# One fp32 product with 136 columns turns a merged block and gives its router logits, and two pieces of TensorE's order move

## The reference

```python
# attention half, x is (8, 1024, 256)
g1 = sigmoid(out_swa @ lin1.T)
g2 = sigmoid(out_mem @ lin2.T)
x = x + (g1 * out_swa + g2 * out_mem)
# expert half
h = layernorm(x)
logits = h @ gate_w.T + gate_b            # 8 experts
topk_prob, topk_idx = top_k(softmax(logits), 2)
pos = cumsum(one_hot(topk_idx)) - 1       # place in the expert's buffer, 1280 places
# gather into the buffers, relu MLP of each expert, weighed sum back onto x
```

## Time and profile before

| | |
|---|---|
| median of 3 runs | 2372.16 us (2371.49 to 2372.21) |
| profiled execution | 2377.75 us, its span 2375.9 us |
| PE busy | 2334.7 us, 98% of the span |
| PE weight loads | 2081.5 us, 88%, beside the products |
| DVE busy | 1689.6 us, 71% |
| ACT busy | 1608.0 us, 68% |
| POOL busy | 1390.1 us, 59% |
| merge phase | about 1392 to 1912 us from the start of the span |

### The profile page before, as it was taken

The page is one execution under the profiler, slowest core; times in us unless marked ns, Lnnn a source line. Parts: engine busy times, 40 slices in busy tenths (PEclk is TensorE's granted clock), DMA queues, the critical chain, the costliest instruction groups (busy, mean ns, idle before and its releaser), DMA issues. The chain is left out here.

```text
span 2375.9 us, 40039 instructions
## 1 busy us (share of the span) xinstructions
PE 2334.7 (98%) x14847; PEld 2081.5 (88%) x14847; DVE 1689.6 (71%) x3668; ACT 1608.0 (68%) x2459; POOL 1390.1 (59%) x1000
## 2 busy tenths in 40 slices
PE   7999999999999999999999999999999899999999
PEld 6888888788888888888888978888888789999999
DVE  7777786666666666666666677777777757777776
ACT  4787888757777777777777657777777545555443
POOL 3565566566776666666667734666666553333433
PEclk9999999999999999999999999999999999999999
DMA  4222221543332223222233322333322055555651
GB/s 130 86 86 72 90 81 54 202 134 69 69 74 63 63 63 67 63 62 63 66 69 66 88 92 87 106 103 101 97 90 75 14 152 153 139 140 150 149 143 60
DMA packets 295394, 221.74 MB, mean 93 GB/s; under 512 B 189282, under 2 KB 262023, under 8 KB 295072
## 3 DMA queue, kind: packets, MB, share of 16 engines
q1 hardware_dynamic: 281376, 188.74, 29.3%
q0 software_dynamic: 13824, 30.44, 4.3%
HBM read 113.30 MB, written 72.12 MB: 78 GB/s over the span
## 5 line engine op out<-in xcount | busy, mean ns | idle before, releaser
L2780 ACT ACTIVATE e_hf<-e_ps_z,e_b 128x640 f32<-128x640 f32 x128 | 101.8, 795 | 211.9 <-PE e_ps_z L105 180.6
L2504 POOL TENSOR_TENSOR m_hl<-m_hf,m_hh 128x512 fp32r<-128x512 f32 x112 | 159.2, 1444 | 103.8 <-ACT m_hh L2103 102.4
L2908 POOL DMA_INDIRECT out<-e_ys,slot_token x80 | 83.2, 1040 | 218.8 <-DVE e_ys L2859 213.2
L105 PE MATMUL e_ps_y<-r_w_h,e_hl 128*128 128x256 f32 x640 | 180.6, 282 | 0.0
L105 PE MATMUL e_ps_y<-r_w_l,e_hh 128*128 128x256 f32 x640 | 179.2, 280 | 0.0
L105 PE MATMUL e_ps_y<-r_w_h,e_hh 128*128 128x256 f32 x640 | 178.9, 280 | 0.0
L1686 POOL TENSOR_TENSOR halves_l<-hT_full,halves_h 128x512 fp32r<-128x512 f32 x120 | 153.4, 1301 | 38.7 <-ACT halves_h L1337 38.7
L932 POOL DMA_INDIRECT xbuf_d<-xn,scatter_rows x128 | 135.8, 1061 | 57.7 <-issue 36.2
L789 POOL TENSOR_TENSOR prob<-prob,softmax_small 128x1024 f32<-128x1024 f32 x65 | 123.2, 1895 | 71.1 <-DVE softmax_small L705 71.1
L105 PE MATMUL e_ps_z<-slotsT_h,w_l 128*128 128x320 f32 x512 | 159.2, 311 | 2.1 <-DVE slotsT_l L2837 2.1
L105 PE MATMUL e_ps_z<-slotsT_l,w_h 128*128 128x320 f32 x512 | 159.1, 311 | 0.0
(11 more groups left out here) (371 smaller groups left out, 8969.5 us busy)
## 6 DMA issues: line engine op xcount, KB each, us to landing
shared_xT<-xT_d SPq DMA_DIRECT2D x64, 256.0 KB, 3.6
new_w1T<-in_W SPq DMA_DIRECT2D x16, 1024.0 KB
new_w2T<-in_W SPq DMA_DIRECT2D x16, 1024.0 KB
xbuf_d<-new_w1T SPq DMA_DIRECT2D x16, 650.0 KB, 8.4
shared_x<-in_x SPq DMA_DIRECT2D x16, 512.0 KB, 4.3
xn_d<-xn SPq DMA_DIRECT2D x32, 256.0 KB, 2.4
xT_d<-shared_xT SPq DMA_DIRECT2D x32, 256.0 KB, 2.6
oT_d<-shared_oT SPq DMA_DIRECT2D x32, 256.0 KB, 2.6
```

The costliest lines, as they stand in the source:

```text
L105: i = e.matmul(out, a, b, start=first and not onto and n == 0, stop=last and n == len(terms) - 1, skip_group_check=onto)
L2504: e.tensor_tensor(hl[:, t, 0:N], hf[(HC * C + t) % NZ][:, 0:N], hh[:, t, 0:N], ALU.subtract).then_inc(*h_low(C, t))
L2780: e.activation(hf[(HC * i + t) % NHF][:].rearrange("p (s n) -> p s n", s=2), ps_z[t % 2][:, :, 0:HALF], ACTF.Relu, bias=b1[:, i % E, t:t + ...
L2908: e.indirect_dma_start(io["out"], bass.IndirectOffsetOnAxis(ap=token[i % 2][:, b:b + 1], axis=0), ys[:, b], None, bounds_check=NT - 1, oob ...
```

## The change

The transposes and the small router products become one plain fp32 product for each of the 8 pairs of block and half. Its moving operand is a new tile `turned` (printed `ident_and_gate`): 128 columns of the identity and the 8 columns of the centred gate, for each half k. It writes 136 columns into a unit of 171 columns of a three-bank PSUM tile `m_ps_t`. The identity columns of a unit are the turned block; the 8 gate columns of the two halves have to be added, which DVE does with a new `sum_logits`. This holds for chunks 0 to 14. Chunk 15 keeps the old way.

Moved are: `residual_router(C-1)` stands behind `gate1(C)`, where `residual` and `router` stood ahead of it; `dispatch(C-2)` stands behind `memory_out(C, 0, 0)`, where it stood ahead of it; ACT's `copy_x1(C-1)` stands behind both `gate1` sigmoids. `dispatch(C)` on TensorE waits in addition for `x1_made` and `lg_summed` of the chunk behind. SP issues two more DMAs of the identity, behind the gate weights and ahead of the other constants.

```diff
         x2 = sb("xn2_full", [P, GRP, D])
-        gate_c, ones_f = sb("gate_centred", [P, KC, E]), sb("m_ones_f", [P, P])
+        turned = sb("ident_and_gate", [P, KC, P + E])
+        gate_c, ones_f = turned[:, :, P:], sb("m_ones_f", [P, P])
...
-        ps_r = ps("m_ps_r", [P, GRP, D])
-        ps_s = ps("m_ps_s", [P, 512])
-        ps_l, ps_c = ps_s[:, 0:GRP * E], ps_s[:, GRP * E:]
+        ps_t = ps("m_ps_t", [P, 3 * 512])
+        units = ps_t[:, 0:GRP * KC * UNIT].rearrange("p (j k x) -> p j k x", k=KC, x=UNIT)
+        ps_r = ps_t[:, 0:GRP * D].rearrange("p (j d) -> p j d", j=GRP)
+        ps_l, ps_c = ps_t[:, GRP * KC * UNIT:GRP * KC * UNIT + GRP * E], ps_t[:, GRP * KC * UNIT + GRP * E:]
...
-        merged_T, logits_done = (signal(n, tails) for n in ("merged_T", "logits_done"))
+        merged_T = signal("merged_T", tails)
+        logits_done = signal("logits_done", [u for u in tails if u[0] == NCH - 1])
+        turned_in = signal("m_turned_in", range(KC), 16)
+        lg_summed = signal("m_lg_summed", chunks[:-1])
...
+            def residual_router(C):
+                pe.wait_ge(*merged.at(C, 0))
+                for k in range(KC):
+                    pe.wait_ge(*turned_in.at(k))
+                pe.wait_ge(*gate_centred.at(0))
+                pe.wait_ge(*x1_made.at(*final_part(C - 1)))
+                if C:
+                    pe.wait_ge(*lg_summed.at(C - 1))
+                if C >= 2:
+                    pe.wait_ge(*placed.at(C - 2, 1))
+                for j in range(SIZES[C]):
+                    for k in range(KC):
+                        i = e.matmul(units[:, j, k, 0:P + E], ga[:, k, j * P:(j + 1) * P], turned[:, k], start=True, stop=True)
+                i.then_inc(*merged_T(C, 0))
...
-                pe.wait_ge(*lg_scaled.at(C))
+                if C < NCH - 1:
+                    read = min(C + 1, NCH - 2)
+                    pe.wait_ge(*x1_made.at(read, 0))
+                    pe.wait_ge(*lg_summed.at(read))
+                else:
+                    pe.wait_ge(*lg_scaled.at(C))
...
@@ -2059,15 +2087,14 @@
                     gate2(C - 1)
                 for t in range(2, HC):
                     hidden(C, t)
+                gate1(C)
                 if tail:
-                    residual(C - 1, 0)
-                    router(C - 1, 0)
-                gate1(C)
+                    residual_router(C - 1)
                 if C == 0:
                     sum_gate()
+                memory_out(C, 0, 0)
                 if sent:
                     dispatch(C - 2)
-                memory_out(C, 0, 0)
                 memory_out(C, 0, 1)
                 memory_out(C, 1, 0)
                 if C == NCH - 1:
...
-                e.activation(x1[s][:, blocks], ps_r[:, blocks], ACTF.Copy).then_inc(*x1_made(C, n))
+                if C < NCH - 1:
+                    e.activation(x1[s][:].rearrange("p j (k d) -> p (j k) d", k=KC),
+                                 units[:, :, :, 0:P].rearrange("p j k d -> p (j k) d"), ACTF.Copy).then_inc(*x1_made(C, n))
+                else:
+                    e.activation(x1[s][:, blocks], ps_r[:, blocks], ACTF.Copy).then_inc(*x1_made(C, n))
...
                 round_hidden(C, 6)
                 round_hidden(C, 7)
                 if tail:
-                    copy_x1(C - 1, 0)
                     gate1(C, 0)
                 gate1(C, 1)
+                if tail:
+                    copy_x1(C - 1, 0)
...
+            def sum_logits(C):
+                dve.wait_ge(*merged_T.at(C, 0))
+                dve.wait_ge(*x1_made.at(C, 0))
+                dve.wait_ge(*chosen.at(C - 1, 0))
+                dve.wait_ge(*shifted.at(C - 1, 0))
+                e.tensor_reduce(lg[:], units[:, :, :, P:P + E].rearrange("p j k x -> p j x k"), AX.X, ALU.add).then_inc(*lg_summed(C))
+
             def router(C):
                 n, wide = SIZES[C], [P, SIZES[C], E]
                 src = ps_l.rearrange("p (j x) -> p j x", x=E)
-                dve.wait_ge(*logits_done.at(*final_part(C)))
                 dve.wait_ge(*gate_b_in.at(0))
-                dve.wait_ge(*chosen.at(C - 1, 0))
-                dve.wait_ge(*shifted.at(C - 1, 0))
+                if C < NCH - 1:
+                    src = lg[:]
+                    dve.wait_ge(*lg_summed.at(C))
+                else:
+                    dve.wait_ge(*logits_done.at(*final_part(C)))
+                    dve.wait_ge(*chosen.at(C - 1, 0))
+                    dve.wait_ge(*shifted.at(C - 1, 0))
...
                 if tail:
+                    sum_logits(C - 1)
                     norm_stats(C - 1, 0)
                 if sent:
                     dispatch(C - 2)
...
             load_oT(0)
             load_x(0)
             e.dma_start(gate[:], io["gateT"].rearrange("(c p) n -> p c n", p=P)).then_inc(*gate_in(0))
+            for k in range(KC):
+                e.dma_start(turned[:, k, 0:P], io["ident"]).then_inc(*turned_in(k))
             e.dma_start(gate_b[:], io["gate_b"]).then_inc(*gate_b_in(0))
             e.dma_start(ident[:], io["ident"]).then_inc(*ident_in(0))
```

More of the change, by code:

```diff
@@ L1812, in gradient_phase @@
         sems.give_back(made)
+UNIT = 171
 def merge_banks():
```

## The result

| | before | after |
|---|---|---|
| median | 2371.35 us (10 runs, 2369.63 to 2372.21) | 2377.64 us (10 runs, 2375.34 to 2378.91) |
| ratio | | 1.0028, 95% interval 1.002 to 1.0036 |
| profiled execution | 2377.75, span 2375.9 | 2376.94, span 2375.1 |

The change makes the kernel slower by 6.3 us. The forecast was 2380.5: a sum of 8.4 on top of the median of the first three runs, 2372.16, and 9.1 above the median of all ten. So the comparison is made stretch by stretch, and the first experiment profiles the kernel before once more.

The account below looks back on a forecast made before the run. TensorE, busy 98% of the span, was taken to bound the kernel. Added were 5.7 us for 15 chunks, 1.4 at `gate2`, 0.95 at the start and 0.4 at the end: 8.4 on 2372.16, giving 2380.5, range 2375.2 to 2386.0.

Parts of the forecast that it names:

- The mechanism: Merge loop: TensorE sets the period; cheaper products save 0.56 us a chunk, but the order makes it 0.38 longer.
- The wait for the sigmoid: TensorE ahead of the memory output: stands still for ACT's first-gate sigmoid, 0.03 + 0.59 + 0.15, 0.77 us.
- the drain: TensorE after the last new product: that instruction's drain delays the memory output by 0.15 us.
- the counting: Counting products behind the first memory output: they keep their present price, 0.25 us a chunk.
- The new products: TensorE in each merge chunk: sixteen fp32 instructions of 136 columns, starting 0.126 us apart, take 2.01 us.
- DVE: DVE in each merge chunk: `norm_stats` and the small work behind it start 1.6 us late.
- Its price at `gate2`: TensorE at `gate2`: waits for DVE's `rest_om`, 0 to 0.25 us, taken as 0.1 a chunk, 1.4 over 14.
- The memory output: TensorE's second memory product, with the counting behind it: 6.27 us against 5.89, 0.38 longer in each of 15 chunks.
- The start: Start of the merge phase: two more DMA issues ahead of `lin1` delay the chain by 0.95 us.
- The bound of 0: Landing of the `lin1` DMA: the least delay is 0, if traffic sets the landing instead.
- The end: Last chunk: ACT's rounding of the last memory output, 2.6 us behind TensorE, may come later; 0.4 taken.
- The profile's own time: Whole profiled execution: 2377.75 us would become 2386.2, keeping its distance of 5.6 above the median.

Follow-up runs that it names:

- the first experiment: The unchanged kernel from before the change, profiled a second time; the execution took 2369.69 us.
- two tiles: The changed kernel in its own order, with separate merged-sum tiles for odd and even chunks; one execution took 2365.11 us.
- The best version: The changed kernel with the 136-column product ahead of the first gate and ACT's copy between the two sigmoids; 2359.28 us against 2370.56, ratio 0.9953.

## Why the prediction was right, and where its terms were off

**The mechanism was right.** TensorE carries the loop, the merged product is cheaper than what it replaces, and the order takes more than that back. With two tiles and nothing else changed the period falls from 30.96 to 29.99; the product, placed ahead of the first gate and with the copy between the sigmoids, gains 0.8 a chunk. The order alone costs 0.94 (31.57), and nothing once nobody waits (30.62).

**The wait for the sigmoid** was put at 0.77 and is 0.78, 15 times. Its parts hold too: 0.04 to ACT (0.03), the drain 0.17 (0.15), the counting 0.26 (0.25).

**The new products** were put at 2.01 and take 1.85. The step that was mis-sized is the pace at 272 column steps, which I took from float32r products, 0.44 ns a column and their overhead. That an instruction streams its columns twice is right: 136 and 160 columns give 0.1158 and 0.1358, which is 2N at 2.4 GHz plus 2.5 ns. The Trainium skill's count (FP8 and Floating Point Precision, TensorE Precision Notes) gave 1.81, nearer than my rows. With the 2.5 ns per matmul that the Trainium skill (TensorE: Matmul & The Clock Gate, Wait — 56ns, not 53.3ns?) measures for bf16 products, the estimate for the sixteen is 1.85. The trace agrees, with its 1.85.

**DVE** was put 1.6 late and is 1.5. Its price at `gate2` was put at 0.1 a chunk and is 0.06 in most, and 0.25 more in two. The memory output was put 0.38 later and comes 0.23 later; the difference is the products' 0.16. So most periods are 0.32 longer where 0.48 was forecast, and the 14 distances 4.85.

**The start** was put at 0.95 and costs nothing. I took an issue's delay for a landing's. `lin1` landed 4.04 after its issue before, and ACT uses it 2.94 after the issue now: in these two profiles the two issues ahead of it don't put off its landing. The bound of 0 that I named was the right end. That traffic sets it was not tested.

**The end** was put at 0.4. From zero of the last chunk to the first product of `gate2_part` it is 18.84 in the kernel before once more (1861.86 to 1880.70) and 20.00 after (1867.03, which is 1869.79 less the first gate's 2.76, to 1887.03). Of these 1.2 the loop's own 0.3 was counted. The other 0.9 is DVE's. Its last rounding, in the kernel before once more, and then after the change, with the product that waits for it:

```profile
1879.89 0.75 DVE L2283 SCALAR_TENSOR_TENSOR keys_l<-m_ps_o,new_b,keys_h 128x512 fp32r<-128x512 f32 x1
```

```profile
1886.23 0.74 DVE L2315 SCALAR_TENSOR_TENSOR keys_l<-m_ps_o,new_b,keys_h 128x512 fp32r<-128x512 f32 x1
1887.03 0.39 PE L105 MATMUL m_ps_z<-keys_h,keys_l 128*128 128x256 f32 x1 [2.53 <-DVE keys_l L2315]
```

From zero it starts at 18.03 before and 19.20 after, behind the small work that started 1.5 late. So I looked at ACT and a gap that wasn't the kernel's, and the late engine was DVE.

**The profile's own time.** I took the execution's distance to its median as fixed. It was that execution's own: of the 8.1 by which it exceeds the second profile of the same kernel, 2.5 are the gap at the end of the merge phase, 4.3 lie in the expert phase, and 1.2 in smaller pieces. The number wasn't touched, since the sum was set on the median.

Loop 4.85 and end 1.2 make 6.0 of the measured 6.3. In the profile after, the expert phase takes 0.9 longer besides than in the kernel before once more, which is less than the 4.3 by which it varies within that kernel.

**Luck.** The loop was put 2.0 too high, mostly by the new products. The start was put 0.95 too high and the end 0.5 too low. Each was wrong by itself, and that they cancel in part is luck.

## What to carry to other kernels

A saving on the engine that sets the end is worth what it is only where the next instruction is ready. Before placing a product last ahead of a stage, ask who overwrites what it reads: here one tile's last reader stood directly ahead of the stage that needed the bank of that tile's next writer. And when the leading engine gets faster, the order on its helpers, which was hidden, has to be looked at again. The best version needed the sigmoid ahead of the copy.

## What the runs showed of the hardware

The granted clock falls without a long pause. An idle 0.83 behind 16 narrow fp32 instructions and 8 transposes was followed by 3.4 us at 1.2 GHz in six of 14 chunks of 31.6 us, and 2.5 behind the 136-column product in every chunk but the first that had it. Within the loop none followed 0.78 or 1.69 behind that product, nor the narrow products without the pause. Each fall cost 1.55 us. So nearly the same wait had two prices: 1.55 us more in six of 14 chunks with the old products, and nothing more with the new one. The length of the wait isn't the reason, since 1.69 behind the new product lowered nothing. Which difference between the products matters was not tested. A plain fp32 instruction starts no sooner than every 0.112 with 8 columns, and every 0.1158 with 136: between these the wider product is nearly free.
